# Moving the scatter of token numbers and the expert tiles of a fused attention and mixture-of-experts kernel to earlier chunks

## Chip, cores and metric

One Trainium2 chip; the program runs on one of its cores. The metric is the device time of one execution in microseconds (us). Before the change the median of three runs is 2175.53 us (2170.86 to 2176.36).

## What is computed

```python
xn = layernorm(x)                       # x: 4 x 2048 x 256, float32
q, k, v = split(xn @ W_qkv.T + b_qkv)   # 16 heads of 16
p = softmax(q @ k.T / 4 - slope[h] * |i - j|)
s = (p @ v) @ W_out.T + b_out
# 8 experts, each token goes to 2 of them, chosen by sigmoid scores within one of two groups
comb = weights of the two chosen experts, normalised
routed = sum over e of comb[:, e] * ((silu(xn @ w_gate[e]) * (xn @ w_up[e])) @ w_down[e])
shared = (silu(xn @ sw_gate) * (xn @ sw_up)) @ sw_down
out = x + s * silu(routed + shared)
```

## The kernel before

Three stages run one after the other. `tokens_stage` (to 292 us) makes the layer norm, q, k, v, the router's logits and the shared expert. `attend_stage` (292 to 2060 us) is where the change lies. `deliver_stage` projects the heads and writes the result.

**Attention sets the pace of the stage.** The scores of the 64 heads (4 batches of 16) are cut into chunks, 428 for each batch, numbered 0 to 427 in a batch. A chunk is up to 1024 columns of scores of one tile of 128 keys. `scores` (PE, L1225) writes it into one of two PSUM slots, ScalarE's exp (L1332) reads it out into SBUF, VectorE (`fade`, L1358) weights the diagonal block, and after the chunks of a step (1 or 2 of them) `weighted_sum` (PE, L1248) multiplies the step before with v. PE makes the scores two chunks ahead, so a chunk's scores wait for the exp of the chunk two before. Heads 0 to 7 have windows and narrower chunks; heads 8 to 15 have 32 chunks each, all of 1024 columns. Head 4 has chunks 56 to 79, head 5 chunks 80 to 107, head 8 begins at 172, head 11 at 268, head 13 at 332.

**Other work is written between the chunks**, in each engine's own order, by chunk number:
- Routing on VectorE (`route`), from chunk 64 of batch 0. It ends with each token's two places in a list sorted by expert.
- The scatter of token numbers (`sort_tile`, POOL, L1159): 64 blocks of tokens with two indirect DMAs each write rows of 64 bytes into the DRAM list `order`. Block t waits for the exp of the chunk that `sort_at(t)` gives, spread evenly from `SORT_FROM` to `SORT_TO`, in hundredths of a batch of columns.
- Then POOL waits for all scatters to land, and loads the list in two halves (L1192) into one buffer. PE turns each half at the chunks `ORDER_AT` (`turn_order`, L1262), and the second load waits for the first turn. VectorE makes integers of it (`take_order`, L1389).
- 72 expert tiles of 256 places. POOL gathers weights (L1164) and tokens (L1168) ahead and stores results (L1173). A tile has four places, each at a step of two chunks: PE turns the tokens (`turn_tile`, L1271), then `gate_up` for gate and for up (L1281), then `down` (L1287). VectorE takes the turned tokens one chunk after the turn (`take_tile`, L1382, L1384), makes the hidden values two chunks after up (`gated`, L1396, L1399), and copies the result one chunk after down (`take_y`, L1406). The places are spread evenly over all steps between `FF_FROM` and `FF_TO`.
- From 3.33 batches on, POOL gathers each token's two results (`fetch`, L1181) and VectorE adds them up (`mix`).

At chunk 68 of batches 1 to 3 (half of head 4) VectorE also turns the next K (L1346) and inverts the sums of the batch before (`reciprocals`, L951 to L957). From chunk 80 of batch 1 (head 5) it makes one step of `guard` (L1423 to L1437) per chunk, eight in all. Within a chunk VectorE's order is: fade, routing, order, read-out, turn of K, reciprocals, guard, take, hidden, y.

The places of the tiles are worked out so:

```python
FF_GAPS = [NC * b + st.chunks[0] for b in range(B) for st in STEPS if len(st.chunks) > 1
           and FF_FROM * BATCH <= 100 * ENDS[NC * b + st.chunks[0]] < FF_TO * BATCH]
ff_gap = lambda n: FF_GAPS[n * len(FF_GAPS) // (4 * TILES_IN)]
sort_at = lambda t: chunk_at((SORT_FROM * NT + (SORT_TO - SORT_FROM) * t) * BATCH // (100 * NT))
```

Of the kernel before, what the change touches and what calls it, by code (L numbers as in the profile page):

```python
# [43 lines left out]
SLOTS_IN = TILES_IN * TILE_IN  # L44
WGU = 2 * DC * I
WROW = WGU + D
FF_FROM, FF_TO = 82, 328
NUMBER = 16
SORT_FROM, SORT_TO = 22, 74
ROUTE_FROM = 64  # L50
PREFIX_AT = 86
ORDER_AT = (350, 356)
FF_PARTS = {"turn": (0, 0), "take": (0, 1), "gate": (1, 0), "up": (2, 0), "tanh": (2, 1), "hid": (2, 2), "down": (3, 0), "y": (3, 1)}
MIX_FROM, MIX_TO = 333, 393
BIAS = 1 + 3 * HD
# [921 lines left out]
def attend_stage(nc, a, keep):  # L977
# [28 lines left out]
    with ExitStack() as ctx:  # L1006
# [97 lines left out]
        with nc.Block() as block:  # L1104
# [101 lines left out]
            def _(pe):  # L1206
# [46 lines left out]
                def prefixes():  # L1253
                    pe.wait_ge(route_loaded, 16 * len(route_loads))
                    pe.wait_ge(marked, 1)
                    flags = chosen[:].rearrange("p t e -> p (t e)")
                    pe.matmul(TY[:], earlier[:], flags, start=True, stop=True)
                    pe.matmul(GU[:].rearrange("p n k -> p (n k)"), every[:], flags, start=True, stop=True).then_inc(prefixed, 1)

                def turn_order(t):  # L1260
                    pe.wait_ge(order_in, 16 * (t + 1))
                    pe.transpose(TY[:, t * TILES_IN:(t + 1) * TILES_IN], order[:, :, 0], ident[0:TILES_IN, 0:TILES_IN]).then_inc(order_turned, 1)  # L1262
# [30 lines left out]
                for b in range(B):  # L1293
                    for s in range(NS):
                        for c in STEPS[s].chunks:
# [4 lines left out]
                            if b == 0 and c == PREFIX_AT:  # L1300
                                prefixes()
                            if b == 0 and c in ORDER_AT:
                                turn_order(ORDER_AT.index(c))
                            for i in ff_due("turn", NC * b + c):
# [33 lines left out]
            def _(dve):  # L1338
# [48 lines left out]
                def take_order():  # L1387
                    dve.wait_ge(order_turned, 2)
                    v.tensor_copy(row_of[:].rearrange("p t i -> p (t i)"), TY[:, 0:2 * TILES_IN]).then_inc(order_ready, 1)  # L1389
# [166 lines left out]
                for n in range(BH):  # L1556
# [3 lines left out]
                    for i, c in enumerate(chunks):  # L1560
                        if CHUNKS[c].folds:
                            fade(b, c)
                        if b == 0 and c >= ROUTE_FROM:
                            next(routing, None)
                        if b == 0 and c == ORDER_AT[1]:
                            take_order()
# [1409 lines left out]
```

## Time and profile before

| | us |
|---|---|
| median of three runs | 2175.53 (2170.86 to 2176.36) |
| the profiled execution, its own time | 2176.23 |
| its span | 2174.1 |
| PE busy | 1931.2 (89%) |
| ScalarE (ACT) busy | 1759.5 (81%) |
| VectorE (DVE) busy | 974.2 (45%) |
| POOL busy | 593.7 (27%) |
| exp of the scores, L1332 (1712 instructions) | 1495.3 |

The span is 2.1 us shorter than the execution's own time. Busy times are over the whole span, so they don't say what bounds a stretch; for that the profile's windows are read stretch by stretch. PE's granted clock is given as a share of 2.4 GHz: 1.00 is that level, and 0.5 is 1.2 GHz.

### The profile page before, as it was taken

How to read it: one execution, taken by the hardware profiler on the slowest of the kernel's cores; microseconds unless marked ns; L12 is line 12 of the kernel's file. 1: busy time of each engine (PE TensorE's matmuls, PEld its weight loads, DVE VectorE, ACT ScalarE, POOL GpSimd, SP SyncE). 2: the span in 40 equal slices, each digit the busy share in tenths (PEclk: the TensorE clock that was granted, in tenths of full speed). 3: DMA queues.
4: the chain of work that ended last, by engine and by line, in shares of the span. 5: the costliest groups of instructions: out<-in, count | busy, mean ns of one | idle time of the engine just before them, and what ended most of it. 6: DMA issues, size and time to landing. Idle time of an engine off the chain costs nothing. (4 is left out here: it accounts for less than half of the span.)

```text
span 2174.1 us, 41264 instructions
## 1 busy us (share of the span) xinstructions
PE 1931.2 (89%) x15804; PEld 683.9 (31%) x15804; DVE 974.2 (45%) x2306; ACT 1759.5 (81%) x2132; POOL 593.7 (27%) x618
## 2 busy tenths in 40 slices
PE   2989997888889989999999999999999998888887
PEld 1655642111112333333333333333333331111133
DVE  4878757411113464333334533333335443444355
ACT  2878777889998877888888878888888789999933
POOL 1322300355532113222222022222221115555100
PEclk7999998999999999999999999999999999999999
DMA  9767752211224444343334433333334334344383
GB/s 317 230 218 248 234 141 63 52 43 42 54 63 123 107 115 120 96 115 92 112 95 115 121 104 108 102 106 104 103 107 130 93 98 115 107 122 117 114 268 134
DMA packets 197717, 269.02 MB, mean 124 GB/s; under 512 B 84800, under 2 KB 153728, under 8 KB 196992
## 3 DMA queue, kind: packets, MB, share of 16 engines
q1 hardware_dynamic: 160064, 171.68, 28.7%
q0 software_dynamic: 29008, 86.28, 13.2%
q10 hardware_dynamic: 8448, 8.39, 1.1%
q8 instruction: 129, 2.11, 0.4%
q14 instruction: 68, 0.56, 0.1%
HBM read 181.69 MB, written 92.69 MB: 126 GB/s over the span
## 5 line engine op out<-in xcount | busy, mean ns | idle before, releaser
L1332 ACT ACTIVATE probs_att<-SC_att 128x1024 f32<-128x1024 f32 (+10 forms) x1712 | 1495.3, 934 | 199.9 <-PE SC_att L1225 177.9
L1248 PE MATMUL O_att<-probs_att,V_att 128*32 128x512 f32 (+7 forms) x8192 | 893.1, 503 | 16.8 <-DVE probs_att L1358 15.3
L1358 DVE TENSOR_TENSOR probs_att<-probs_att,decay 128x128 f32<-128x128 f32 x1024 | 293.5, 291 | 894.5 <-ACT probs_att L1332 829.3
L1225 PE MATMUL SC_att<-Q,K_turned_att 64*128 64x512 f16 (+7 forms) x2152 | 457.3, 336 | 69.0 <-ACT probs_att L1332 52.2
L1225 PE MATMUL SC_att<-Q,K 64*128 64x512 f16 (+7 forms) x2020 | 413.1, 326 | 52.8 <-ACT probs_att L1332 33.6
L1225 PEld LDWEIGHTS SC_att<-Q,K_turned_att 64*128 64x128 f16 x2152 | 128.4, 93 | 811.3 <-ACT probs_att L1332 550.4
L1173 POOL DMA_DIRECT2D ys<-ys_att x72 | 54.4, 755 | 784.6 <-DVE ys_att L1406 784.6
L1248 PEld LDWEIGHTS O_att<-probs_att,V_att 128*32 128x32 f32 x8192 | 165.5, 108 | 225.8 <-issue 180.4
L1159 POOL DMA_INDIRECT order<-ids_att,place x128 | 123.7, 966 | 211.0 <-ACT probs_att L1332 179.7
L1225 PEld LDWEIGHTS SC_att<-Q,K 64*128 64x128 f16 (+1 forms) x2020 | 122.6, 94 | 138.8 <-ACT probs_att L1332 78.6
L1168 POOL DMA_INDIRECT x<-xn,row_of_att x144 | 139.6, 969 | 70.4 <-PE TY_att L1271 37.3
L1181 POOL DMA_INDIRECT x<-ys,place x128 | 124.9, 975 | 107.8 <-ACT probs_att L1332 61.2
L1281 PE MATMUL GU_att<-xT_att,x 128*128 128x256 f16 x864 | 121.3, 277 | 9.9 <-issue 9.7
L635 POOL TENSOR_TENSOR inverse<-qk_tok,inverse 128x512 f16<-128x512 f32 x64 | 75.0, 1182 | 187.5 <-ACT inverse L669 179.8
L533 PE MATMUL GU_tok<-xT_tok,w_qkv_tok 128*128 128x512 f16 x384 | 90.7, 387 | 17.5 <-DVE xT_tok L854 17.5
L1287 PE MATMUL TY_att<-x,hid_att 128*128 128x256 f32 x288 | 81.4, 405 | 14.2 <-DVE hid_att L1399 14.0
L1281 PEld LDWEIGHTS GU_att<-xT_att,x 128*128 128x128 f16 x864 | 73.8, 98 | 46.4 <-issue 36.9
L1164 POOL DMA_INDIRECT x<-w_rows,owner x72 | 71.2, 988 | 28.8 <-issue 23.3
L1406 DVE COPY ys_att<-TY_att 128x512 f32<-128x512 f32 x72 | 49.8, 691 | 65.0 <-PE TY_att L1287 65.0
L1665 ACT ACTIVATE z_del<-Z_del,b_all_del 128x512 f32<-128x512 f32 x32 | 22.0, 688 | 62.7 <-PE Z_del L1704 62.7
L1322 ACT ACTIVATE th_att<-GU_att,halve_att 128x256 f32<-128x256 f32 x72 | 34.2, 474 | 47.2 <-PE GU_att L1281 47.1
L1382 DVE TENSOR_SCALAR xT_att<-TY_att 128x512 f16<-128x512 f32 x72 | 49.7, 690 | 44.4 <-PE TY_att L1271 41.9
(184 smaller groups left out, 1436.3 us busy)
## 6 DMA issues: line engine op xcount, KB each, us to landing
K<-k_stack SPq DMA_DIRECT2D x128, 256.0 KB
Q<-q_stack SPq DMA_DIRECT2D x128, 256.0 KB
ys<-ys_att POOLq DMA_DIRECT2D x72, 256.0 KB
x<-in_x SPq DMA_DIRECT2D x24, 512.0 KB, 6.3
k_stack<-inverse SPq DMA_DIRECT2D x96, 128.0 KB
q_stack<-inverse SPq DMA_DIRECT2D x96, 128.0 KB
xn<-x_tok SPq DMA_DIRECT2D x16, 512.0 KB, 6.2
values<-v_block_tok SPq DMA_DIRECT2D x16, 512.0 KB, 5.4
```

The source lines that it names most:

```text
L533: mm = pe.matmul(GU[:, m, :], w_qkv[:, w, c, m * P:(m + 1) * P], xT[:, j % 2, x, c, :], start=(k == 0), stop=(k == len(PRODUCTS) - 1))
L635: nc.gpsimd.tensor_tensor(parts[:, k, 1, :], qk[:, m, :], parts[:, k, 0, :], ALU.subtract).then_inc(part2, 1)
L1159: nc.gpsimd.indirect_dma_start(keep["order"], index(keep["place"][:, n, t:t + 1]), ids[:, t, :], None).then_inc(sorted_out, 16)
L1164: nc.gpsimd.indirect_dma_start(w[:, i % 3, :], None, keep["w_rows"], index(keep["owner"][:, i:i + 1])).then_inc(w_in[i % 3], 16)
L1168: nc.gpsimd.indirect_dma_start(xs[:, i % 2, t, :], None, keep["xn"], index(row_of[:, t, i:i + 1])).then_inc(xs_in[i % 2], 16)
L1181: nc.gpsimd.indirect_dma_start(pairs[:, t % 4, n, :], None, keep["ys"], index(keep["place"][:, n, t:t + 1])).then_inc(mix_in[t % 4], 16)
L1225: mm = pe.matmul(SC[:, c % SLOTS, at:at + x1 - x0], K[par][side or 0][rows, k * P:(k + 1) * P], Q[par][rows, x0:x1], start=True, stop=True)
L1248: mm = pe.matmul(O[VW * g:VW * (g + 1), par, col:col + width * len(mine)], V[par][:, k, :], spans[:, j0:j0 + BPB * (len(mine) - 1) + 1:BPB ...
L1281: mm = pe.matmul(GU[:, n, :], w_of(i, wp, c, n), xT[:, xp, c, :], start=(k == 0), stop=(k == len(PRODUCTS) - 1))
L1287: mm = pe.matmul(TY[:, t * D:(t + 1) * D], hid[:, t * P:(t + 1) * P], w[:, i % 3, WGU:WROW], start=True, stop=True)
L1332: nc.scalar.activation(probs[chunk.step % DEPTH][:, chunk.base:chunk.base + chunk.width], SC[:, c % SLOTS, start:start + chunk.width], ACT ...
L1358: v.tensor_tensor(diag, diag, decay[:, chunk.head, :], ALU.mult).then_inc(faded, 1)
```

## The change

Four numbers change. Places between 0.66 and 3.28 batches in place of 0.82 and 3.28 are open to expert tiles. The last block of the scatter is due at 0.58 batches in place of 0.74, with the same start at 0.22. PE turns the halves of the list at chunks 289 and 295 in place of 350 and 356.

```diff
-FF_FROM, FF_TO = 82, 328
+FF_FROM, FF_TO = 66, 328
-SORT_FROM, SORT_TO = 22, 74
+SORT_FROM, SORT_TO = 22, 58
-ORDER_AT = (350, 356)
+ORDER_AT = (289, 295)
```

Worked out from `FF_GAPS`: 436 steps before and 467 now are open for the 288 parts of the 72 tiles. The first tile's turn, gate, up and down stand at chunks 360, 362, 366, 368 of batch 0 before, and at 298, 300, 304, 306 now. The last tile's parts stand at chunks 138, 142, 144 and 148 of batch 3, before and now. The parts by batch, those in heads 8 to 15 and those in heads 4 to 7:

| batch | wide heads 8 to 15, before | now | heads 4 to 7, before | now |
|---|---|---|---|---|
| 0 | 23 | 41 | 0 | 0 |
| 1 | 85 | 79 | 34 | 32 |
| 2 | 85 | 79 | 34 | 32 |
| 3 | 0 | 0 | 27 | 25 |

The instructions of each engine stay the same; on POOL and SP their order does too. On PE, the place where the second half of the list is turned and the first tile follows (L1262 turns the list, L1271 the tile's tokens, L1225 are scores, L1248 weighted sums). Before:

```order
L1262 MATMUL TY_att<-ident,x 128x72
L1225 MATMUL SC_att<-Q,K_turned_att 128x512
L1225 MATMUL SC_att<-Q,K_turned_att 128x256
L1225 MATMUL SC_att<-Q,K 128x256
L1248 MATMUL O_att<-probs_att,V_att 32x512 x4
L1225 MATMUL SC_att<-Q,K_turned_att 128x512 x3
L1225 MATMUL SC_att<-Q,K_turned_att 128x384
L1225 MATMUL SC_att<-Q,K 128x128
L1248 MATMUL O_att<-probs_att,V_att 32x512 x4
L1225 MATMUL SC_att<-Q,K_turned_att 128x512 x2
L1271 MATMUL TY_att<-ident,x 128x128 x4
```

Now:

```order
L1262 MATMUL TY_att<-ident,x 128x72
L1248 MATMUL O_att<-probs_att,V_att 32x512 x4
L1225 MATMUL SC_att<-Q,K_turned_att 128x512 x4
L1248 MATMUL O_att<-probs_att,V_att 32x512 x4
L1225 MATMUL SC_att<-Q,K_turned_att 128x128
L1225 MATMUL SC_att<-Q,K 128x512
L1225 MATMUL SC_att<-Q,K 128x384
L1271 MATMUL TY_att<-ident,x 128x128 x4
```

From the list's second turn to the first tile's turn there were four chunks' scores, and now there are three.

On VectorE, the middle of head 4 in batch 1, from the turn of the next K (L1346) through the reciprocals (L951 to L957) to the expert tile's next part. Before:

```order
L1346 TENSOR_SCALAR K_turned_att<-K,turn 128x2048
L951 RECIPROCAL recip<-sums_in 128x256
L952 TENSOR_TENSOR least<-least,recip 128x256
L953 TENSOR_TENSOR most<-most,recip 128x256
L954 CAST recip_parts<-recip 128x256
L955 TENSOR_TENSOR recip<-recip,recip_parts 128x256
L956 CAST recip_parts<-recip 128x256
L957 TENSOR_TENSOR recip_parts<-recip,recip_parts 128x256
L1358 TENSOR_TENSOR probs_att<-probs_att,decay 128x128 x2
L1396 SCALAR_TENSOR_TENSOR hid_att<-th_att,GU_att 128x256
L1399 SCALAR_TENSOR_TENSOR hid_att<-GU_att,halve_att,hid_att 128x256
L1358 TENSOR_TENSOR probs_att<-probs_att,decay 128x128
```

Now:

```order
L1346 TENSOR_SCALAR K_turned_att<-K,turn 128x2048
L951 RECIPROCAL recip<-sums_in 128x256
L952 TENSOR_TENSOR least<-least,recip 128x256
L953 TENSOR_TENSOR most<-most,recip 128x256
L954 CAST recip_parts<-recip 128x256
L955 TENSOR_TENSOR recip<-recip,recip_parts 128x256
L956 CAST recip_parts<-recip 128x256
L957 TENSOR_TENSOR recip_parts<-recip,recip_parts 128x256
L1396 SCALAR_TENSOR_TENSOR hid_att<-th_att,GU_att 128x256
L1399 SCALAR_TENSOR_TENSOR hid_att<-GU_att,halve_att,hid_att 128x256
L1358 TENSOR_TENSOR probs_att<-probs_att,decay 128x128
L1406 COPY ys_att<-TY_att 128x512
```

The hidden values (L1396, L1399) stood two chunks behind the reciprocals, and now stand right behind them, in the same chunk; PE's down of that tile, which waits for them, was at chunk 72 and is now at chunk 68.

The same place in batch 2. Before:

```order
L1346 TENSOR_SCALAR K_turned_att<-K,turn 128x2048
L951 RECIPROCAL recip<-sums_in 128x256
L952 TENSOR_TENSOR least<-least,recip 128x256
L953 TENSOR_TENSOR most<-most,recip 128x256
L954 CAST recip_parts<-recip 128x256
L955 TENSOR_TENSOR recip<-recip,recip_parts 128x256
L956 CAST recip_parts<-recip 128x256
L957 TENSOR_TENSOR recip_parts<-recip,recip_parts 128x256
L1358 TENSOR_TENSOR probs_att<-probs_att,decay 128x128
L1382 TENSOR_SCALAR xT_att<-TY_att 128x512
L1384 SCALAR_TENSOR_TENSOR xT_att<-TY_att,xT_att 128x512
```

Now:

```order
L1346 TENSOR_SCALAR K_turned_att<-K,turn 128x2048
L951 RECIPROCAL recip<-sums_in 128x256
L952 TENSOR_TENSOR least<-least,recip 128x256
L953 TENSOR_TENSOR most<-most,recip 128x256
L954 CAST recip_parts<-recip 128x256
L955 TENSOR_TENSOR recip<-recip,recip_parts 128x256
L956 CAST recip_parts<-recip 128x256
L957 TENSOR_TENSOR recip_parts<-recip,recip_parts 128x256
L1358 TENSOR_TENSOR probs_att<-probs_att,decay 128x128
L1396 SCALAR_TENSOR_TENSOR hid_att<-th_att,GU_att 128x256
L1399 SCALAR_TENSOR_TENSOR hid_att<-GU_att,halve_att,hid_att 128x256
```

The two instructions that take the turned tokens (L1382, L1384) stood behind the reciprocals and now stand ahead of them. In batch 3 it was the copy of the result (L1406) that stood behind them; now a take stands ahead of them and the next part, the hidden values, six chunks later.

## Rows read from the trace of the kernel before

**Rows 1.** Windows, exp instructions (L1332) alone; columns: stretch, length, ACT busy (count), PEclk, DMA share, GB/s

```profile
451.40:617.50 166.10, 148.16 (x157) 0.97 0.20 46
617.50:638.10 20.60, 20.60 (x23) 1.00 0.43 94
896.70:1152.00 255.30, 215.68 (x225) 1.00 0.36 105
```

**Rows 2.** The same view, from the stage's start: how many exps had begun by then

```profile
292.00:575.40 283.40, 239.84 (x290) 0.93 0.25 58
```

**Rows 3.** Timeline of POOL: scatters, list loads, first gathers; columns: start, us, work, [idle before]

```profile
403.42 1.21 POOL L1159 DMA_INDIRECT order<-ids_att,place  x1 [120.60 <-ACT probs_att L1332]
404.94 0.97 POOL L1159 DMA_INDIRECT order<-ids_att,place  x1 [0.30 <-issue]
406.21 0.96 POOL L1159 DMA_INDIRECT order<-ids_att,place  x1 [0.30 <-issue]
...
616.56 0.96 POOL L1159 DMA_INDIRECT order<-ids_att,place  x1 [0.30 <-issue]
618.95 0.64 POOL L1192 DMA_DIRECT2D x<-order  x1 [1.43 <-DMA order<-ids_att,place]
640.49 0.54 POOL L1192 DMA_DIRECT2D x<-order  x1 [20.90 <-PE TY_att L1262]
646.54 1.03 POOL L1164 DMA_INDIRECT x<-w_rows,owner  x1 [5.50 <-DVE row_of_att L1389]
...
649.15 0.95 POOL L1168 DMA_INDIRECT x<-xn,row_of_att  x1 [0.30 <-issue]
```

**Rows 4.** Lines L1159 and L1192: duration min/median/max in ns; landing of the list loads

```profile
L1159 POOL DMA_INDIRECT order<-ids_att,place x128: 953/960/1212, 403.4 to 616.6; - x128
...
DMA to landing us min/median/max: 5.0/5.6/6.1
```

**Rows 5.** Timeline of PE: the first tile's turn

```profile
652.04 0.66 PE L1271 MATMUL TY_att<-ident,x 128*128 128x128 f32 x4 [2.72 <-DMA x<-xn,row_of_att]
```

**Rows 6.** Windows: head 4, then head 5, of batches 1, 2, 3; PE, PEld, DVE, ACT, POOL busy, PEclk, DMA

```profile
774.40:797.00 22.60, 19.92 (x210) 7.70 (x210) 13.04 (x33) 16.41 (x25) 5.36 (x6) 1.00 0.46 122
1231.90:1258.90 27.00, 21.53 (x212) 7.84 (x216) 13.37 (x34) 16.82 (x27) 3.80 (x4) 0.87 0.32 84
1692.60:1718.20 25.60, 21.80 (x212) 7.99 (x208) 12.56 (x32) 16.71 (x25) 3.63 (x4) 0.87 0.39 89
797.00:828.70 31.70, 26.93 (x238) 9.89 (x238) 20.26 (x37) 21.02 (x31) 7.79 (x8) 0.89 0.35 98
1258.90:1286.60 27.70, 25.12 (x238) 9.57 (x233) 11.16 (x28) 20.91 (x30) 7.34 (x8) 1.00 0.46 124
1718.20:1744.20 26.00, 24.78 (x234) 9.49 (x238) 11.69 (x29) 20.91 (x30) 7.49 (x8) 1.00 0.45 124
```

**Rows 7.** Timeline of DVE in batch 2, chunk 68: turn of K, reciprocals, take

```profile
1242.67 0.75 DVE L1346 TENSOR_SCALAR K_turned_att<-K,turn 128x2048 f16<-128x2048 f16 x1
1243.33 1.75 DVE L951 RECIPROCAL recip<-sums_in 128x256 f32<-128x256 f32 x1
...
1247.02 0.43 DVE L957 TENSOR_TENSOR recip_parts<-recip,recip_parts 128x256 bf16<-128x256 f32 x1
...
1248.41 0.69 DVE L1384 SCALAR_TENSOR_TENSOR xT_att<-TY_att,xT_att 128x512 f16<-128x512 f32 x1
```

**Rows 8.** Timeline of PE: tile parts that waited, in batches 1, 2 and 3

```profile
805.46 0.80 PE L1281 MATMUL GU_att<-xT_att,x 128*128 128x256 f16 x3 [3.74 <-issue]
...
1249.20 1.01 PE L1281 MATMUL GU_att<-xT_att,x 128*128 128x256 f16 x4 [3.81 <-issue]
...
1708.86 0.87 PE L1271 MATMUL TY_att<-ident,x 128*128 128x128 f32 x3 [2.65 <-DVE ys_att L1406]
```

**Rows 9.** Timeline of DVE in batch 1, head 5: a guard step, the take

```profile
799.59 1.21 DVE L1425 TENSOR_TENSOR o<-o 16x1024 f32<-16x1024 f32 x1
...
804.67 0.69 DVE L1384 SCALAR_TENSOR_TENSOR xT_att<-TY_att,xT_att 128x512 f16<-128x512 f32 x1
```

## The prediction

> **What bounds the kernel now.** The change touches only the attention stage, so I read that stage in windows, exp instructions first, because ScalarE's exp is the one engine whose work per chunk never changes in the wide heads. Right behind the last scatter and ahead of the first tile, ScalarE is busy for all of a stretch of 20.60 us that touches 23 exps [rows 1]. A count takes in the exps cut by both ends, so that is 22 chunks of 0.94 us. That is the floor. With expert tiles between the chunks it is 255.30 us for 224 chunks, 1.14 us each; with scatters beside them 166.10 us for 156, 1.065 us each, at a mean clock of 0.97 [rows 1]. So both kinds of side work cost time: a tile (about 12.1 chunks long before the change, 288 parts on 436 steps) costs 12.1 x 0.20 = 2.4 us, and a chunk beside scatters costs 0.13 us. The question is whether the change removes any of either, since it only moves them.
>
> Then I read the timelines of POOL, PE and VectorE at the four places where a moved part meets something fixed: the list's loads, the first tile, and heads 4 and 5 of batches 1 to 3.
>
> **The change part by part**, against the profiled execution's own 2176.2 us (0.7 us above the median, 2175.5).
>
> 1. *The tiles themselves.* There are 72 before and after, ending at the same place. Parts in wide heads go from 193 to 199, in heads 4 to 7 from 95 to 89. A part costs 2.4 / 4 = 0.6 us in a wide head. The six leave heads where no row prices them alone: between nothing and the same 0.6. So the sum is between 0 and +3.6 us; in head 5 alone 8 parts of batches 2 and 3 stand in 27.70 and 26.00 us at ScalarE's 20.9 us busy [rows 6], so those chunks are far from ScalarE's floor and PE's added work is paid there as well. I take the term near its lower end: **+0.5**. POOL's extra gathers in batch 0 hide beside the exps (it has nothing else to do there, 20 us of idle ahead of its second list load, [rows 3]).
>
> 2. *The scatters.* 128 indirect DMAs, issued from 403.42 to 617.5 us now, mostly held back by the exp they wait for. Free ones follow each other at 1.27 us (404.94 to 406.21, [rows 3]). 128 x 1.27 = 162 us, so the last would end at about 566 us, where the table has it due at chunk 266, near 551: POOL cannot keep the new pace, and runs flat out. The stretch beside scatters then ends near 566 us in place of 617.5, some 48 chunks sooner. If a chunk in their company costs 0.13 us whatever their rate, that is -6 us. If each scatter costs its share of the stretch's 156 x 0.13 = 20 us, it is 0, since all 128 still run. The rows don't tell the two apart, and part of the 20 us is a lowered clock after short idle times: I take the middle, **-3**, and keep both ends. Against it: the Trainium skill's page SBUF — State Buffer, section "SBUF: two separate sides", says that engine ports and DMA ports are disjoint and neither slows the other; by that rule the scatters are not what slows the chunks, the term is 0 and the sum below ends 3 us higher. The second row of [rows 1], the floor reached as soon as they stop, speaks the other way, though in one short stretch.
>
> 3. *The list's first half.* Its load starts 1.43 us behind the last scatter and lands 6.1 us after its issue [rows 3, 4], so at about 566 + 1.4 + 6.1 = 574 us; with a delay like the few that POOL shows in 213 us, 576 to 577. PE wants it at chunk 289, which is 575.4 us and a little now (290 exps begun by then, [rows 2]). Before, the half lay ready for 15 us. The wait is between 0 and 3 us: **+0.5**. All queued behind it on PE is the attention itself, so a wait here is paid in full. The second half keeps its six chunks (5.0 us of load, [rows 3, 4]), as before: 0.
>
> 4. *The first tile.* PE's turn stood four chunks behind the list's second turn and waited 2.72 us for the tokens [rows 5]; POOL's chain from the list to the tokens' landing (646.54, 649.15 us, [rows 3]) is the same. Now three chunks are between, one floor chunk of 0.94 us less cover: **+0.9**, 0 to +2. Gate, up and down follow at the same distances.
>
> 5. *Head 4.* At chunk 68 VectorE is blocked for 4.8 us (1242.67 to 1247.45, [rows 7]) by the turn of K and the reciprocals. A tile's part that needs VectorE just then holds up PE. Batch 1 has none there now and head 4 takes 22.60 us at full clock; in batch 2 gate waits 3.81 us for the take behind the block, and head 4 takes 27.00 us at clock 0.87; in batch 3 the turn waits 2.65 us, 25.60 us [rows 6, 8]. After the change batches 2 and 3 are free of it: -4.0 and -3.0. Batch 1 gets the worst place: down at chunk 68 waits for hidden values of the same chunk, behind the block: 4.8 us and 0.9 for the two instructions, less what PE lags. By batch 2's price (3.8 us of wait cost 4.4) **+4.5**. Sum **-2.5**; ends: -7 (batch 1 free) and +1.
>
> 6. *Head 5 of batch 1.* Guard steps of 1.2 us fill VectorE, the take comes out at 805.4, and gate waits 3.74 us [rows 8, 9]. Head 5 takes 31.70 us, against 27.70 and 26.00 in batches 2 and 3 [rows 6]. Now turn and gate stand at chunks 90 and 94, clear of the guard; up at 84 and down at 88 lie within it, and down needs hidden values. **-2.5**, between 0 and -4.
>
> Sum: +0.5 - 3 + 0.5 + 0.9 - 2.5 - 2.5 = **-6.1 us**, so **2170.1 us**, 5.4 us (0.25%) below the median. About 0.3%, or 6.5 us, is what a measurement of this kernel can tell from no change; the forecast lies just inside it.
>
> **Rivals.**
> - *Only the waits move (scatters cost by number, or not at all).* Term 2 is 0 and the others stand: 2173 us. For it: the same 128 scatters run, only closer together.
> - *The long gain.* The scatters cost by time (-6), batch 1's down finds its values (PE may reach it late, since scores and sums of chunk 68 come first), and head 5 loses all of its 4 us: +0.5 - 6 + 0.9 - 7 - 4 = -15.6, or 2160.6 us at its end; half way to it from the forecast, about 2165 us, is what I give this case. For it: in heads 4 and 5 two of the three large waits certainly lose their cause.
> - *The list comes too late (slower).* PE meets the empty buffer at chunk 289. It decides at a mean of (576.3 - 7.5 - 403.4) / 128 = 1.29 us per scatter; each 0.01 us above that costs 1.3 us in full. At 1.40 us, PE waits 14 us: 2176.2 - 6.6 + 14 = 2184 us. For it: full rate over 160 us is shown nowhere, and the margin was 15 us and is now 2. Against it: 1.27 us in [rows 3]. The skill's SBUF page, same section, says that descriptors of a POOL DMA can't be written while VectorE holds the shared port in a two-port mode; the turn of K (0.75 us, [rows 7]) is such a candidate once per head. Worked out from rows, five heads x 0.75 us = 3.7 us later: a wait of 2 to 4 us at chunk 289, 2173 us. But of 128 scatters none takes over 1.21 us, median 0.96 [rows 4], with these turns among them, so I give this rule little.
> - *It doesn't do what it says.* POOL can't keep 0.36 batches, as term 2 shows; the list and the tiles do move, since PE's own order moves them.
>
> **Chances.** Forecast's own case 0.40 (2170 us, its own range 2166 to 2174), waits only 0.20, long gain 0.30, late list 0.10. Faster by over 0.3% (below 2169): all of the long gain and 0.12 of the first case, 0.42. Slower by over 0.3%: the late list, 0.10. Within: 0.48. The range reaches down to the long gain's end and up past the waits-only case to a list some 6 us late: 2161 to 2178 us.
>
> **What would show it.** The scatters end at 565 to 569 us and start 1.27 us apart. PE's first L1262 waits under 2 us; the first L1271 waits about 3.6 us. Head 4 of batches 2 and 3 takes about 23 us at clock 1.00, that of batch 1 about 27 us with a wait at L1287. Head 5 of batch 1 takes about 29 us. A tile in the wide heads still costs 2.4 us. Chunks beside scatters at 1.06 us speak for cost by time, at 1.10 for cost by number. A first L1262 that waits over 5 us, or a tile that costs under 2.2 us when spread wider, would make the forecast wrong.

## The result, and the profile after

The changed kernel takes 2227.38 us (median of four runs, 2224.28 to 2230.33), against 2175.39 us before (four runs): a ratio of 1.025, 95% interval 1.0233 to 1.0267. It is slower by 52 us, where 5 us less was forecast and 2178 us was the upper end. The profiled execution took 2230.33 us, its span is 2228.3 us.

To see where, cut the attention stage by chunks. The table is made from the starts of the 1712 exps, in us; a stretch reaches from the start of one chunk's exp to that of the other.

| batch, chunks | what stands there | before | after | difference |
|---|---|---|---|---|
| 0, 0 to 123 | attention, routing | 110.4 | 110.1 | -0.3 |
| 0, 123 to 172 | scatters | 48.9 | 64.7 | +15.8 |
| 0, 172 to 268 | scatters | 102.3 | 146.3 | +44.0 |
| 0, 268 to 298 | scatters before (they end at chunk 326), list after | 31.4 | 29.1 | -2.4 |
| 0, 298 to 310 | scatters before, first tile after | 11.6 | 23.9 | +12.3 |
| 0, 310 to 428 | tiles; first tile before | 134.3 | 132.2 | -2.1 |
| 1, head 4 (56 to 80) | down beside the reciprocals | 22.6 | 27.5 | +4.9 |
| 1, head 5 (80 to 108) | guard | 31.7 | 31.2 | -0.5 |
| 1, heads 6 to 15 | 7 parts fewer | 360.1 | 354.9 | -5.2 |
| 2, heads 4 and 5 | | 54.7 | 48.2 | -6.5 |
| 2, heads 6 to 15 | 7 parts fewer | 361.7 | 354.7 | -7.0 |
| 3, heads 4 and 5 | | 51.7 | 51.1 | -0.6 |

So the loss is in batch 0, beside the scatters: +59.8 us between chunks 123 and 268. The +12.3 us of chunks 298 to 310 are not the price of an earlier first tile, since the first tile before stands in the next row. Like for like, the 12 chunks from the first tile's turn take 21.0 us before (360 to 372) and 23.9 us now (298 to 310), 2.9 us more. From chunk 298 to the last exp the changed kernel gains 3.3 us in all.

The exps in windows (columns as in [rows 1]), chunks 172 to 268 before:

```profile
451.40:553.70 102.30, 91.07 (x97) 0.97 0.21 48
```

The same chunks of the changed kernel, and the stretch behind them:

```profile
466.70:613.00 146.30, 91.75 (x98) 0.82 0.15 35
613.00:632.00 19.00, 18.51 (x20) 0.96 0.34 84
```

ScalarE's work is unchanged, but it is idle for 54.6 of 146.3 us, where it was idle for 11.2 of 102.3, and PE's mean clock is 0.82. In the last row the scatters have ended at 612 us, and the pace is back near the floor at once. How one of the lost pieces looks, in the timelines of ScalarE, PE and POOL:

```profile
525.66 1.02 ACT L1332 ACTIVATE probs_att<-SC_att 128x1024 f32<-128x1024 f32 x1 [0.85 <-issue]
530.66 2.85 ACT L1332 ACTIVATE probs_att<-SC_att 128x1024 f32<-128x1024 f32 x3 [3.97 <-remote]
...
525.24 0.39 PE L1225 MATMUL SC_att<-Q,K_turned_att 64*128 64x512 f16 x2
525.31 0.32 PE L1225 MATMUL SC_att<-Q,K 64*128 64x384 f16 x1
526.74 0.39 PE L1225 MATMUL SC_att<-Q,K 64*128 64x512 f16 x2 [1.11 <-issue]
527.06 1.07 PE L1248 MATMUL O_att<-probs_att,V_att 128*32 128x512 f32 x8
531.74 0.61 PE L1225 MATMUL SC_att<-Q,K_turned_att 64*128 64x512 f16 x2 [3.61 <-ACT probs_att L1332]
...
519.20 0.96 POOL L1159 DMA_INDIRECT order<-ids_att,place  x1 [3.43 <-ACT probs_att L1332]
520.46 0.96 POOL L1159 DMA_INDIRECT order<-ids_att,place  x1 [0.30 <-issue]
...
526.96 0.95 POOL L1159 DMA_INDIRECT order<-ids_att,place  x1 [0.50 <-issue]
528.22 0.96 POOL L1159 DMA_INDIRECT order<-ids_att,place  x1 [0.31 <-issue]
532.87 0.96 POOL L1159 DMA_INDIRECT order<-ids_att,place  x1 [3.70 <-ACT probs_att L1332]
```

The exp that starts at 530.66 us is that of chunk 212, and PE had written its scores by 525.63 us (the pair of lines at 525.24 and 525.31). PE then wrote the next chunk's scores (to 527.13) and a weighted sum (to 528.1). From there both engines stand still for 2.5 us with nothing between them in the program.

The profile puts ScalarE's wait down to "remote", which means that it found no instruction whose end fits the semaphore update that released it. The trace also keeps the times of these updates, which no view prints. PE's increments for the scores finished at 525.63 and at 527.13 are there at 530.636 and 530.679 us, and that of the weighted sum of 528.1 at 530.771: three increments within 0.14 us, the first of them 5.0 us late. ScalarE's exp starts 0.02 us behind its increment. The ends of matmuls are modelled, but PE had started two later groups (at 526.74 and 527.06) before the first of these increments came. So what ScalarE waits for is PE's signal, and not PE's work.

Over chunks 123 to 332, 40 of the increments for scores come over 0.5 us behind the last scores that PE had finished (at most 5.4 us by this count), while no increment of ScalarE's exps or VectorE's fade comes later than 0.012 us. Counted by ScalarE: ahead of 22 exps it stands idle for over 0.5 us although their scores had been finished over 0.5 us before, 58.6 us together. In 14 of the 22 (50.0 us) the view says "remote". In the kernel before there are 28 such increments (at most 1.6 us) and 13 such exps, 14.8 us together. The view names PE's scores for 12 of them, and only one is called "remote", which was there to be read:

```profile
461.18 1.02 ACT L1332 ACTIVATE probs_att<-SC_att 128x1024 f32<-128x1024 f32 x1 [2.05 <-remote]
```

The list and the first tile, which answer to [rows 3, 5]:

```profile
611.38 0.96 POOL L1159 DMA_INDIRECT order<-ids_att,place  x1 [0.31 <-issue]
615.68 0.64 POOL L1192 DMA_DIRECT2D x<-order  x1 [3.33 <-DMA order<-ids_att,place]
635.15 0.54 POOL L1192 DMA_DIRECT2D x<-order  x1 [18.84 <-PE TY_att L1262]
641.32 1.03 POOL L1164 DMA_INDIRECT x<-w_rows,owner  x1 [5.62 <-DVE row_of_att L1389]
...
642.38 1.09 SPq L966 DMA_DIRECT2D K<-k_stack  x2
643.51 1.24 SPq L966 DMA_DIRECT2D Q<-q_stack  x2
...
651.72 1.11 PE L1271 MATMUL TY_att<-ident,x 128*128 128x128 f32 x4 [8.06 <-DMA x<-xn,row_of_att]
```

The scatters end at 612 us, five us sooner than before in place of fifty. The list lies ready for PE, since chunk 289 is late by more than the list. But the first tile's tokens take 10 us from the first gather to PE's turn, where they took 5.5 before, and SyncE's loads of the next head's K and Q (1 MB) are issued in the same two us.

Heads 4 and 5 of batches 1 to 3 after, as [rows 6]:

```profile
842.50:870.00 27.50, 21.89 (x212) 8.07 (x216) 12.70 (x32) 16.85 (x25) 3.68 (x4) 0.88 0.32 83
1300.20:1323.40 23.20, 20.61 (x225) 7.78 (x224) 13.84 (x34) 16.73 (x25) 5.66 (x6) 1.00 0.42 107
1746.50:1772.00 25.50, 21.38 (x210) 8.26 (x207) 13.25 (x33) 16.77 (x26) 5.82 (x6) 0.93 0.39 100
870.00:901.20 31.20, 27.01 (x228) 9.97 (x232) 19.50 (x36) 20.83 (x30) 6.50 (x7) 0.89 0.32 93
1323.40:1348.40 25.00, 23.12 (x215) 8.74 (x215) 10.31 (x26) 20.77 (x30) 3.98 (x5) 1.00 0.39 101
1772.00:1797.50 25.50, 23.93 (x233) 8.88 (x227) 10.47 (x27) 20.75 (x30) 5.59 (x6) 1.00 0.56 126
```

The slow head 4 has moved from batch 2 to batch 1, where PE's down waited 4.4 us for the hidden values, as the order of instructions had it.

### The profile page after: what moved, and what is told of

It reads as the page before. It is cut to its first block and busy times, and to the rows that moved or that the text cites. A ratio compares the mean times of both kernels' runs of the same rounds, so it can differ in the third digit from the quotient of the medians.

```text
span 2228.3 us, 41266 instructions
## 1 busy us (share of the span) xinstructions
PE 1953.7 (88%) x15804; PEld 687.5 (31%) x15804; DVE 972.6 (44%) x2306; ACT 1760.0 (79%) x2132; POOL 593.3 (27%) x618
## 3 DMA queue, kind: packets, MB, share of 16 engines
q0 software_dynamic: 29008, 86.28, 13.1%
## 5 line engine op out<-in xcount | busy, mean ns | idle before, releaser
L1332 ACT ACTIVATE probs_att<-SC_att 128x1024 f32<-128x1024 f32 (+10 forms) x1712 | 1495.8, 934 | 248.9 <-PE SC_att L1225 173.5
L1248 PE MATMUL O_att<-probs_att,V_att 128*32 128x512 f32 (+7 forms) x8192 | 907.2, 510 | 20.3 <-DVE probs_att L1358 17.6
L1225 PE MATMUL SC_att<-Q,K_turned_att 64*128 64x512 f16 (+7 forms) x2152 | 460.0, 339 | 105.1 <-ACT probs_att L1332 82.3
L1225 PE MATMUL SC_att<-Q,K 64*128 64x512 f16 (+7 forms) x2020 | 417.2, 331 | 51.2 <-ACT probs_att L1332 30.9
L1225 PEld LDWEIGHTS SC_att<-Q,K_turned_att 64*128 64x128 f16 x2152 | 128.2, 93 | 860.4 <-ACT probs_att L1332 591.5
L1248 PEld LDWEIGHTS O_att<-probs_att,V_att 128*32 128x32 f32 x8192 | 166.5, 109 | 233.1 <-issue 189.7
L1159 POOL DMA_INDIRECT order<-ids_att,place x128 | 123.8, 967 | 206.1 <-ACT probs_att L1332 169.9
L1225 PEld LDWEIGHTS SC_att<-Q,K 64*128 64x128 f16 (+1 forms) x2020 | 123.6, 95 | 137.7 <-ACT probs_att L1332 75.4
L1406 DVE COPY ys_att<-TY_att 128x512 f32<-128x512 f32 x72 | 49.8, 692 | 71.2 <-PE TY_att L1287 71.2
L1322 ACT ACTIVATE th_att<-GU_att,halve_att 128x256 f32<-128x256 f32 x72 | 34.2, 474 | 51.7 <-PE GU_att L1281 51.7
L1382 DVE TENSOR_SCALAR xT_att<-TY_att 128x512 f16<-128x512 f32 x72 | 49.7, 690 | 48.1 <-PE TY_att L1271 45.4
```

What stands on the lines that cost most here:

```text
L1159: nc.gpsimd.indirect_dma_start(keep["order"], index(keep["place"][:, n, t:t + 1]), ids[:, t, :], None).then_inc(sorted_out, 16)
L1225: mm = pe.matmul(SC[:, c % SLOTS, at:at + x1 - x0], K[par][side or 0][rows, k * P:(k + 1) * P], Q[par][rows, x0:x1], start=True, stop=True)
L1248: mm = pe.matmul(O[VW * g:VW * (g + 1), par, col:col + width * len(mine)], V[par][:, k, :], spans[:, j0:j0 + BPB * (len(mine) - 1) + 1:BPB ...
L1332: nc.scalar.activation(probs[chunk.step % DEPTH][:, chunk.base:chunk.base + chunk.width], SC[:, c % SLOTS, start:start + chunk.width], ACT ...
```

## The experiments

The theory after the result: scatters that are due faster than before hold up PE and ScalarE. The rival: the list or the tiles, earlier, do it. Each time below has its ratio to the kernel before, run beside it (medians of 2184.95, 2184.93, 2191.74 and 2174.23 us, so only ratios compare across experiments). Stretches are read from one profiled execution each. The yardstick below is the time from the start of chunk 123 to that of chunk 332, the stretch of the scatters, which before took 218.8 us.

**The scatter's end alone.**

```diff
-SORT_FROM, SORT_TO = 22, 74
+SORT_FROM, SORT_TO = 22, 58
```

> The kernel before with the scatter's end alone moved, from 0.74 to 0.58 batches; list and tiles stay at chunks 350, 356 and 360 on. Theory (T1): scatters that follow each other without a pause hold up TensorE and ScalarE, and cost about 60 us between chunks 123 and 268: the time is about 2235 us, and chunks 172 to 268 take about 146 us in place of 102. Rival (T2): the slow chunks come from the list or the tiles standing earlier: then this kernel stays at 2175 us.

Measured: 2229.43 us (ratio 1.0194, 1.0146 to 1.0242). Chunks 123 to 332 take 266.3 us, 47.5 more than before; chunks 172 to 268 take 142.6. The exps there:

```profile
465.90:608.50 142.60, 91.92 (x97) 0.83 0.15 36
```

Nearly the row of the changed kernel, with list and tiles at their old places. The rival is out, and this one number makes the change slower.

**The change without its scatters, and the kernel before without them.** The edit in both:

```diff
-                for t in range(NT):
-                    sort_tile(t)
-                pool.wait_ge(sorted_out, 16 * 2 * NT)
```

> The changed kernel without its 128 scatters (left out: the list of token numbers stays zero, so every tile gathers token 0). T1: chunks 123 to 289 run at their floor, and what is left of the change is the wait at the first tile (about 8 us) against the gains further on: about 2150 us. T2: the slow stretch between chunks 123 and 268 stays, over 2200 us.

> The kernel before without its 128 scatters (left out as well; every tile gathers token 0). It prices the scatters at their old pace: T1, with 0.13 us per chunk over some 200 chunks, says 20 to 25 us less than before, about 2152 us. Against the changed kernel without scatters it prices the earlier list and tiles alone: +12 us at the first tile and -17 us later would make this kernel about 5 us slower than that one.

Without scatters every tile gathers token 0, so these kernels show times alone.

Measured: 2151.64 us (ratio 0.9838, 0.9786 to 0.9890) and 2157.24 us (0.9864, 0.9807 to 0.9921), two runs each; the two profiled spans are the same, 2152.2 us. In the old places, chunks 123 to 332 take 191.4 us:

```profile
442.20:532.10 89.90, 89.88 (x97) 1.00 0.19 45
```

That is the floor all along, 0.936 us per chunk, where before it took 1.065. So the scatters cost 218.8 - 191.4 = 27 us where 203 chunks were given to them, and 266.3 - 191.4 = 75 us in the experiment above, with 143 chunks: the cost is neither a fixed one by number nor in proportion to the time in their company. The rest of the change, list and tiles earlier, is worth little: nothing by the spans, 5.6 us less by the medians of two runs each, which such few runs don't tell apart. The first tile is dearer in the new place (the 12 chunks from its turn take 25.7 us against 21.8), and the later stretches give that back.

**The same indirect DMAs, the other way.** The scatter's end at 0.58 and:

```diff
-nc.gpsimd.indirect_dma_start(keep["order"], index(place), ids[:, t, :], None)
+nc.gpsimd.indirect_dma_start(ids[:, t, :] or its spare, None, keep["order"], index(place))
```

(`place` stands for the block's column of places, the spare is the unused `ys`.)

> The scatter's end at 0.58 batches, list and tiles as before, but each scatter turned into a gather of the same 128 rows of 64 bytes from the same list by the same indices (the list stays zero and the token numbers are overwritten, so every tile gathers token 0). If the writes of small rows into DRAM are what costs (T1a): about 2155 to 2175 us, no slow stretch. If it is POOL making indirect DMAs without a pause, whichever way they go (T1b): about 2235 us, chunks 172 to 268 at 146 us.

Measured: 2229.34 us (ratio 1.0193, 1.0147 to 1.0240); chunks 123 to 332 take 267.3 us. It is not that they are writes.

```profile
465.40:610.30 144.90, 92.16 (x97) 0.85 0.18 35
```

**The scatter's end at 0.66, alone.**

```diff
-SORT_FROM, SORT_TO = 22, 74
+SORT_FROM, SORT_TO = 22, 66
```

> The scatter's end alone moved, from 0.74 to 0.66 batches (0.44 batches long; 0.52 cost 22 us over no scatters, 0.36 cost about 80). If the cost grows with the rate along the whole way: about 40 us over none, 18 us slower than before. If it sets in only where POOL has no pause left (128 x 1.27 us = 162 us against 0.44 batches at the floor pace, about 176 chunks x 0.94 = 165 us, still near that edge): nearer to 60 over none, and the slowdown is again in single waits of 3 us and more.

Measured: 2202.64 us (ratio 1.0077, 1.0038 to 1.0115); chunks 123 to 332 take 244.0 us, 53 over none. It lies between the two cases that were expected (40 and near 60), with five "remote" waits of 13.6 us together.

**The scatters one by one, over the old stretch.**

```diff
-                    pool.wait_ge(expd, sort_at(t))
                     for n in range(2):
+                        pool.wait_ge(expd, sort_at(t + n / 2))
```

(In `sort_at` the place is also rounded down to an integer, because of the halves.)

> The kernel before (end at 0.74 batches), with each of a block's two scatters waiting for its own chunk, in place of both at the same one: same number, same mean rate, no pairs. If it is bursts that hurt, the 22 us that the scatters cost fall to under 12 us and the kernel is 10 us faster than before. If it is the mean rate, no change.

Measured: 2179.96 us (ratio 0.9973, 0.9950 to 0.9996); chunks 123 to 332 take 214.5 us, 23 over none in place of 27. Pairs matter little here; what counts is how many chunks the table gives to all of them.

**Plain DMAs of the same bytes.** The scatter's end at 0.58 and:

```diff
-nc.gpsimd.indirect_dma_start(keep["order"], index(keep["place"][:, n, t:t + 1]), ids[:, t, :], None)
+pool.dma_start(keep["order"][(2 * t + n) * P:(2 * t + n + 1) * P, :], ids[:, t, :])
```

> The scatter's end at 0.58 batches, each scatter turned into a plain DMA from POOL that writes the same 128 rows of 64 bytes in a row, to fixed places of the list (so the list is wrong, and the tiles gather by it). If descriptors and writes as such hold up the engines: 2225 us again. If it is what POOL does to make an indirect DMA, each address from an index: the slow stretch goes, below 2185 us.

Measured: 2155.35 us (ratio 0.9868, 0.9814 to 0.9922); chunks 123 to 332 take 191.4 us, as without any. The group of POOL's instructions of the scatter's line (mean, median and largest duration in ns, and from when to when):

```profile
L1159 POOL DMA_DIRECT2D order<-ids_att x128: 537/537/824, 402.6 to 532.4; - x128
```

And the exps in the window that answers to chunks 172 to 268:

```profile
443.50:533.40 89.90, 89.88 (x97) 1.00 0.23 54
```

They ran closer together than any indirect ones (130 us for 128, 1.0 us each), from the same engine, on the same queue with the same 29008 packets over the whole kernel, with the same writes and the same increments of the semaphore, and cost nothing. In the stretch of the scatters the queue's packets are alike too, in the trace's own table: in both kernels half are of 512 bytes and half of 4, 27 ns in the median, though the indirect ones go to scattered rows and the plain ones to rows side by side. So it is not what the DMAs move or where to; what is left is what POOL does to make an indirect one, 0.96 us of work in place of 0.54.

**Half of them in the short stretch.** The scatter's end at 0.58 and:

```diff
-                    for n in range(2):
+                    for n in range(1):
...
-                pool.wait_ge(sorted_out, 16 * 2 * NT)
+                pool.wait_ge(sorted_out, 16 * NT)
```

> The scatter's end at 0.58 batches, list and tiles as before, only the first of each block's two scatters (left out: the second choices' places in the list, which stay zero). 64 indirect DMAs in the short stretch, so a longer pause between them than in any kernel so far. Cost by rate (T1): about as little as at 0.90 batches, under 5 us over no scatters, 2155 to 2160 us. Cost by number and place: half of the 80 us, about 2195 us; half of the old 22 us: 2165 us.

Measured: 2156.62 us (ratio 0.9841, 0.9808 to 0.9873); chunks 123 to 332 take 191.7 us: 64 indirect DMAs, 2.05 us apart, cost 0.3 us.

```profile
445.00:534.80 89.80, 89.80 (x96) 1.00 0.21 49
```

**Where the first tile's wait came from.** The change without scatters, and:

```diff
-FF_FROM, FF_TO = 66, 328
+FF_FROM, FF_TO = 68, 328
```

> The changed kernel without its scatters (left out, as in the earlier run) and tiles from 0.68 batches on: the first turn at chunk 306 in place of 298, that is 11 chunks behind the list's second turn and 8 behind the point where SyncE loads the next head's K and Q. Theory: at 298 the tokens' gather landed beside those loads (1 MB), which made PE wait 9 us and then run at half clock; the waiting goes, and the stretch from chunk 298 to 332 is 10 to 14 us shorter: about 2140 us. Rival: POOL's chain is as slow without the loads; then 306 gains only as many us as it comes later, and the wait is still over 1 us.

Measured: 2158.26 us (ratio 0.9848, 0.9815 to 0.9881). The turn no longer waits (575.22 us, nothing in brackets), and chunks 298 to 332 take 42.7 us in place of 50.2: 7.5 less, not 10 to 14, and a part of that is that two parts fewer stand there. The rest of the expected gain is in the same view of ScalarE: while POOL gathered for the first three tiles in a row, it waited once more for nothing that the program shows.

```profile
570.28 2.85 ACT L1329 ACTIVATE probs_att<-SC_att 128x1024 f32<-128x1024 f32 x3 [2.49 <-remote]
```

And the time as a whole did not fall at all, where 2140 us was expected (its span is 2155.2 us, against 2152.2 with 0.66), because all later tiles moved as well: heads 4 and 5 of batch 2 take 4.5 us more, the heads behind them 4.0, and heads 4 and 5 of batch 3 take 4.6 more. Whether the loads of K and Q alone delayed the tokens isn't settled by it, since the turn has both moved past them and got more time.

**The other direction: a slower scatter and later tiles.**

```diff
-FF_FROM, FF_TO = 82, 328
+FF_FROM, FF_TO = 98, 328
-SORT_FROM, SORT_TO = 22, 74
+SORT_FROM, SORT_TO = 22, 90
-ORDER_AT = (350, 356)
+ORDER_AT = (400, 408)
```

> The other direction: the scatter's end at 0.90 batches (0.68 long), the list at chunks 400 and 408, tiles from 0.98 batches on, so that their parts stand closer together (1.41 steps each, in place of 1.51). The theory (cost by pauseless scatters; a tile costs about 2.45 us wherever it stands) expects the scatters to cost some 8 to 12 us in place of 22 and the rest unchanged: 2160 to 2167 us, faster than before. Rival (closer tiles cost more than they save): at or above 2176 us.

> The kernel with the scatter's end at 0.90, list at 400 and 408 and tiles from 0.98 once more, in more rounds, for the size of its gain: about 1% faster than before, near 2160 us.

Measured: 2161.02 us (ratio 0.9894, 0.9859 to 0.9929), and again 2159.68 us (0.9854, 0.9827 to 0.9881). It is faster than the kernel before, and so than the changed one. Chunks 123 to 332 take 194.6 and 194.4 us, 3 over none, where 8 to 12 were expected. A tile in heads 8 to 15 of batches 1 and 2 costs 2.56 us at 11.3 chunks each, against 2.45 at 12.1 before and 2.35 at 13.0 in the changed kernel (from the exps' starts, over the floor of 0.94 us a chunk): closer tiles cost some 0.1 us more each.

**The same, one by one.** The edit above for single scatters, added to this one.

> The kernel with the scatter's end at 0.90, list at 400 and 408 and tiles from 0.98, and each scatter waiting for its own chunk, so that they stand about 1.9 us apart one by one. If the mean rate is all that counts, it costs as with pairs: within 2 us of that kernel, near 2160 us. If pairs cost on their own, the 3 us that are left of the scatters' cost go too.

Measured: 2150.21 us against 2174.23 of before beside it (ratio 0.9900, 0.9882 to 0.9917). Chunks 123 to 332 take 191.6 us, the floor: the last 3 us of the scatters are gone. Its ratio is not below the two of the version with pairs (0.9894 and 0.9854), so the whole isn't shown to be faster than with pairs; the gain is shown for this stretch alone.

```profile
444.40:534.40 90.00, 89.82 (x96) 1.00 0.21 50
```

The scatters' price in one table. Due spacing: the chunks from the first scatter's number to the last one's, by 0.94 us, over 127 (63 for the half). Measured spacing: from the first one's start (400 to 404 us) to the last one's, over the same. The last column is ScalarE's idle time ahead of exps whose scores had long been finished, counted as above.

| scatter stretch | due spacing, us | last start, us | measured spacing, us | chunks 123 to 332, us | over none | idle behind finished scores, us |
|---|---|---|---|---|---|---|
| none | | | | 191.4 | | 0.0 |
| 0.36, plain DMAs in their place | 1.06 | 532.4 | 1.02 | 191.4 | 0.0 | 0.0 |
| 0.36, half the number | 2.1 | 533.3 | 2.05 | 191.7 | 0.3 | 0.0 |
| 0.68, single | 1.95 | 650.7 | 1.94 | 191.6 | 0.2 | 0.0 |
| 0.68, pairs | 1.95 | 652.3 | 1.96 | 194.6 | 3 | 1.2 |
| 0.52, single | 1.50 | 610.3 | 1.65 | 214.5 | 23 | 13.1 |
| 0.52, pairs (before) | 1.50 | 616.6 | 1.68 | 218.8 | 27 | 14.8 |
| 0.44, pairs | 1.28 | 611.4 | 1.64 | 244.0 | 53 | 37.4 |
| 0.36, pairs | 1.06 | 606.9 | 1.60 | 266.3 | 75 | 51.5 |
| 0.36, gathers in their place | 1.06 | 608.8 | 1.61 | 267.3 | 76 | 54.1 |

Two things stand out. The late signals come and go with the price: where the scatters cost 3 us or less, no increment of PE's scores in the stretch is over 0.5 us late (0.05 us at most without indirect DMAs in it), and where they cost 53 to 76 us, ScalarE's idle time behind finished scores is 37 to 54 us of it. The rest is not split up; PE's lowered clock is in it. And in the five rows at the end, 128 indirect DMAs end at nearly the same moment, 203 to 213 us after the first, however few chunks the table lays over them:

| stretch | chunks given | at the floor, us | first to last scatter, us | of it POOL waits for exps, us | chunks 123 to 332 over none, us |
|---|---|---|---|---|---|
| 0.52 | 203 | 191 | 213 | 59 | 27 |
| 0.44 | 173 | 163 | 209 | 52 | 53 |
| 0.36 | 143 | 134 | 203 | 42 | 75 |

This is not POOL's own pace for 128 of them, since POOL itself waits for exps in 42 to 59 us of it. The last scatter waits for its own chunk, so the time from first to last already holds the loss, and the difference to the floor explains nothing. What goes on is a ring: POOL makes scatters back to back (1.27 us apart) as soon as they are due, PE's signals come late, the exps wait for them, and POOL waits for the exps. That the sum stays near 210 us is what three stretches show, and no cause for it is shown.

## Why the prediction was wrong

1. *The tiles themselves* (+0.5): right in kind. The seven parts fewer in batches 1 and 2 gave 5.2 and 7.0 us, 0.75 to 1 us a part and not 0.6. In sum the list-and-tiles half of the change is worth between 0 and 5.6 us, by the two kernels without scatters.

2. *The scatters* (-3, between -6 and 0): **the step that failed.** The term measures +47.5 us (the scatter's end alone, chunks 123 to 332). It set up two laws, a cost by time and a cost by number, and bounded the term by them, so that a loss stood outside the bounds. Both assume that a chunk or a scatter costs no more when scatters are denser. The runs show a cost that rises steeply with density: 0.3 us for 64 of them 2.05 us apart, 3 us for 128 due 1.95 us apart, 27 us at 1.50, 53 us at 1.28 and 75 us at 1.06. They show where it arises, too: PE's increments reach ScalarE up to 5 us late while POOL makes indirect DMAs, so the attention is not free to run on while POOL catches up. The step said that POOL would run flat out, 1.27 us each and 162 us for all; POOL did so in bursts only and took 208 us, since it waited 49 us for exps that had themselves been held up. The wait of 2.05 us at 461 us, with a lowered clock behind it, and twelve more of its kind were the sign that wasn't read: ScalarE idle although the scores had been finished. By the rule of the Trainium skill's page SBUF — State Buffer, section "SBUF: two separate sides", that engines and DMAs don't slow each other, the scatters would have cost nothing. For plain DMAs the runs agree (0.0 us); for indirect ones the measurement decides, 27 to 75 us. That these come from SBUF ports is not shown.

3. *The list's first half* (+0.5): the wait was 0.2 us, but for another reason, which is luck. POOL's end came at 612 us in place of the 566 worked out, and PE's chunk 289 at 633 in place of 575. The rival of the late list had the right sign and the right engine, POOL slower than 1.27 us in the mean (1.64), and the wrong way to pay for it: not PE waiting at the list, but ScalarE and PE held up all along.

4. *The first tile* (+0.9): like for like 2.9 us (the 12 chunks from its turn, 23.9 against 21.0). The turn waited 8.06 us and not 3.6, since the tokens landed later; the clock fell to half at 648.8 us, within that wait, for 6.8 us. The term took POOL's chain as fixed in length, and it took 5 us more. The next head's loads, which SyncE issues at the same time, are a likely reason, but no run shows it alone.

5. *Head 4* (-2.5): +4.9, -3.8 and -0.2, against +4.5, -4.0 and -3.0. Batches 1 and 2 came out as worked out. In batch 3 the tile was free of the reciprocals, but PE's weighted sum ran into VectorE's fade behind the same block:

```profile
1763.36 0.73 PE L1248 MATMUL O_att<-probs_att,V_att 128*32 128x320 f32 x8 [1.96 <-DVE probs_att L1358]
```

6. *Head 5 of batch 1* (-2.5): -0.5. Gate was clear of the guard, and down, at chunk 88, waited 3.2 us for hidden values within it. The step named this and gave it no price.

The long gain and the waits-only case fell with term 2. The other terms, -3.1 us together, are within what two runs of the kernels without scatters leave open.

## What to carry to other kernels

Where a change gives a background engine less time for the same work, what that work cost before is no bound: its price can rise steeply with its rate. So raise the rate in steps, and look for an engine that stands idle although its producer has finished, which no count of busy time shows. Here the best place for a scatter of indirect DMAs is the longest stretch that the rest allows, one by one and about 2 us apart; tiles packed closer to make room for it cost some 0.1 us more each. And parts moved by a spread-out table land on other fixed work (reciprocals, guard, a head's loads) all along the kernel, so a shift of two hundredths of a batch moved single stretches by 4 to 5 us.

## What the runs showed of the hardware

While POOL made indirect DMAs closely one after the other, the semaphore increments for PE's scores came late, behind the last scores finished by up to 5.4 us in the changed kernel, up to 1.6 us before, and up to 0.05 us without indirect DMAs in the stretch. Those of ScalarE and VectorE stayed within 0.012 us in every one of these runs. ScalarE then stood idle with its scores finished, and the attention went from 0.94 to 1.52 us per chunk (146.3 us for 96), with PE's clock at 0.82 in the mean.

It happened with scatters and gathers alike (128 due 1.06 us apart cost 75 and 76 us), and not with plain DMAs of the same bytes and packets from the same engine and queue at 1.0 us apart (0.0 us). At 1.94 to 2.05 us apart the indirect ones cost 0.2 to 3 us. It was seen once more without scatters, beside the token and weight gathers of three tiles (ScalarE idle for 2.49 us at 570 us, with tiles from 0.68 batches on).

Why PE's increments are late is open. POOL's reads of the indices, its work on the addresses and its writing of descriptors were not told apart.
